# A Macaron layer on one core: the first mixture after two batches' scatters, the late layout between its chunks, the rows written by ScalarE

## The reference

```python
x = x + 0.5 * ffn(layernorm(x))
x = x + attention(layernorm(x))
x = x + 0.5 * ffn(layernorm(x))
# ffn: a mixture of 8 experts, 2 per token
xf = layernorm(x) * ln_g + ln_b
scores, idx = top_k(xf @ router_w, 2); gate = softmax(scores)
# per expert: y = layernorm(xf) * g + b;  x1 = y @ W1 + b1;  x2 = clip(y @ W2 + b2, -20, 20)
# hidden = clip(x1 * x2 * sigmoid(x2), -1e4, 1e4);  out = clip(hidden @ Wo + bo, -1e4, 1e4)
```

## Time and profile before

| | us |
|---|---|
| median of 3 runs | 1285.2 |
| lowest and highest | 1285.19, 1287.82 |
| the profiled execution, whole | 1283.73 |
| its span | 1282.0 |

### The profile page before, as it was taken

One profiled execution on the slowest core, in us unless ns is written; L12 is line 12 of the kernel. 1 busy time (PEld: TensorE's weight loads), 2 busy tenths in 40 slices (PEclk: granted clock), 3 DMA queues, 4 the chain that ended last, 5 costly groups with the idle time before them and its releaser, 6 DMA issues.

```text
span 1282.0 us, 27027 instructions
## 1 busy us (share of the span) xinstructions
PE 1144.8 (89%) x9003; PEld 606.4 (47%) x9003; DVE 1124.8 (88%) x2287; ACT 878.0 (68%) x1849; POOL 518.6 (40%) x672
## 2 busy tenths in 40 slices
PE   3857999888699999999999999999999999999993
PEld 2745888877322222332223223222222367788882
DVE  7877888887799999989999999999999778988885
ACT  1223555555289999898889888898887965455651
POOL 3883556424224001525336333445344128543232
PEclk9999999999689999999999999999999999999997
DMA  8115565563110200012011000010000413555653
GB/s 278 53 63 181 206 204 194 196 238 137 51 51 18 68 18 4 16 31 55 2 31 37 21 18 18 20 42 10 18 9 25 147 72 142 193 206 191 243 200 141
DMA packets 58746, 123.28 MB, mean 96 GB/s; under 512 B 12736, under 2 KB 33954, under 8 KB 58576
## 3 DMA queue, kind: packets, MB, share of 16 engines
q1 hardware_dynamic: 49616, 103.57, 23.6%
q0 software_dynamic: 8704, 16.93, 4.2%
q10 hardware_dynamic: 288, 1.05, 0.2%
HBM read 36.39 MB, written 23.62 MB: 47 GB/s over the span
## 4 chain that ended last, share of the span: by engine, by line
PE 59%; DVE 25%; POOL 6%; issue 5%; DMA 3%; ACT 2%; SPq 1%; DVEq 0%; POOLq 0%; ACTq 0%
PE psum L2329 15%; DVE att_neg_part L1996 13%; PE psum L2301 9%; PE psum L2232 8%; PE psum L2220 7%; PE psum L2222 7%; PE psum L2283 6%; POOL rows_dram L1293 4%; DVE ffn_x2c L1938 2%; DMA ffn_block_rows<-rows_dram 2%; DVE ffn_hidden L1949 2%; DVE stats L1631 1%; PE psum L2307 1%; ACT ffn_silu L1454 1%; PE psum L2172 1%
## 5 line engine op out<-in xcount | busy, mean ns | idle before, releaser
L1996 DVE TENSOR_REDUCE att_neg_part<-psum 128x2 f32<-128x1024 f32 x512 | 594.7, 1215 | 27.0 <-PE psum L2283 24.9
L1486 ACT ACTIVATE att_probs<-psum 128x512 f32<-128x512 f32 x1024 | 556.4, 597 | 59.8 <-PE psum L2301 23.0
L2329 PE MATMUL psum<-att_probs,att_values 128*18 128x256 f32 x4096 | 322.2, 387 | 4.3 <-issue 3.7
L2283 PE MATMUL psum<-att_right,att_left 62*128 62x512 f16 x1024 | 288.1, 391 | 31.0 <-DVE att_neg_part L1996 30.1
L1454 ACT ACTIVATE ffn_silu<-ffn_x2c,ffn_rec 128x256 f32<-128x256 f32 (+1 forms) x320 | 154.7, 487 | 170.4 <-DVE ffn_x2c L1938 169.9
L1309 POOL DMA_INDIRECT y_dram<-ffn_y,ffn_block_rows x144 | 142.6, 990 | 233.9 <-ACT ffn_y L1472 205.5
L2301 PE MATMUL psum<-att_right,att_left 64*128 64x512 f16 x512 | 199.0, 389 | 0.1
L2307 PE MATMUL psum<-att_right,att_left 64*128 64x512 f16 x512 | 194.9, 381 | 0.0
L1938 DVE TENSOR_SCALAR ffn_x2c<-psum,ffn_rec 128x256 f32<-128x256 f32 (+1 forms) x320 | 162.6, 512 | 34.0 <-PE psum L2222 29.7
L2220 PE MATMUL psum<-ffn_block_t,ffn_rec 128*128 128x256 f32 (+1 forms) x640 | 178.7, 361 | 1.8 <-ACT ffn_block_t L1405 1.8
L2222 PE MATMUL psum<-ffn_block_t,ffn_rec 128*128 128x256 f32 (+1 forms) x640 | 178.0, 360 | 0.0
(11 more groups left out here) (236 smaller groups left out, 1040.8 us busy)
## 6 DMA issues: line engine op xcount, KB each, us to landing
ffn_rec<-record SPq DMA_DIRECT2D x80, 776.5 KB, 3.8
ffn_block_rows<-rows_dram SPq DMA_DIRECT2D x64, 130.0 KB, 3.1
record<-in_L_ffn_W SPq DMA_DIRECT2D x16, 256.0 KB, 6.4
att_left<-q_parts_dram SPq DMA_DIRECT2D x64, 64.0 KB, 2.2
att_right<-att_max_parts SPq DMA_DIRECT2D x256, 1.0 KB
y_dram<-ffn_y,ffn_block_rows POOLq DMA_INDIRECT x144, 2.3
x_sb<-in_L_attn_x SPq DMA_DIRECT2D x4, 512.0 KB, 7.1
record<-in_L_ffn_Wo SPq DMA_DIRECT2D x8, 256.0 KB, 7.2
```

The lines of the kernel that those rows point to most:

```text
L1486: S.activation(probs[:, slot % PROBS, :], ring_bank(("score", slot))[:, :], ACT.Exp, scale=unlift).then_inc(att_bank.by_act, 1)
L1996: V.tensor_reduce(out=neg_part[:, h % 2, keys, p::PAIR, t], in_=psum[:, low:high + 1, :], axis=AX.X, op=ALU.max, negate=True).then_inc(red ...
L2283: product = TE.matmul(bank[max_banks(n)[k]], left[s][PRODUCTS[k], p, q], right[s][PRODUCTS[k], p, seen], start=True, stop=True)
L2329: last = TE.matmul(value_bank[g * VS:g * VS + 2 * VW, p * HALF // 2:(p + 1) * HALF // 2], values_flat[:, at:at + 2 * VW], queries, start=( ...
```

## The change

The first mixture starts when the rows of batches 0 and 1 are scattered (`JOBS[0:B - 2]`). The first 9 blocks (`AHEAD`) hold only rows of these two batches: the early layout puts first the whole blocks of `rows_ahead`, and SP waits for batch 2's scatters before it loads block 9. Batch 2's 16 scatters stand at the end of GpSimd's part of the front, and batch 3's remaining ones in slots 0 to 40 of `HEAD`. The late layout moves from the front into `HEAD`, one piece in each of blocks 2 to 10, and the fillers follow it, three a block from block 14 on.

ScalarE writes the rows: `scalar_fill` is 8 activations, one for each tile, Identity with scale rstd and bias -mean * rstd, which VectorE works out as `offset` in one instruction. The semaphore on which the gates wait now counts the fill and the exponent. The pass (x - mean) * ln_g goes from step 0 to step 2, the transposes can start after half of xf, the logits after half of the copies, and the routing uses two PSUM banks per batch in turn. The constants of VectorE stand behind batch 1's statistics. `first_routing` has a new order, written out by batch, folds and scatters included. New buffers and the move of batch 2's and 3's routing buffers behind those of the mixture are left out below, as are unchanged lines.

```diff
@@ -119,6 +119,7 @@
+    AHEAD = -((E * (BLOCK - 1) - TOPK * N * (B - 2)) // BLOCK)
@@ -451,8 +460,9 @@
-        route_bank = [Banks([bank[b]], semaphore(f"route_full{b}"), semaphore(f"route_emptied{b}"))
-                      for b in range(B)]
+        route_banks = [Banks(bank[2 * k:2 * k + 2], semaphore(f"route_full{k}"), semaphore(f"route_emptied{k}"))
+                       for k in range(2)]
+        route_bank = [route_banks[b % 2] for b in range(B)]
@@ -508,7 +518,9 @@
-            return [n for n in range(PLACED + 1) if not (on_pool(job) and n in (XF, FILLED))]
+            if job[0] == 0 and job[1]:
+                return [SHIFTED1, XF_FIRST, XF, SHIFTED2, WON, CHOSEN, LED, FILLED, PLACED]
+            return [n for n in range(PLACED + 1) if not (on_pool(job) and n in (XF, FILLED) or job[0] and n == XF_FIRST)]
@@ -517,8 +529,13 @@
-        def by_act(job, step):
-            return set_of(job).by_act, job[4] * ACT_STEPS + step
+        def rows_by_act(job):
+            return set_of(job).by_act, 1
+        def shared(job):
+            return set_of(job).by_act, 2 + job[4] * ACT_STEPS
@@ -728,10 +745,13 @@
+        OUT_SLOTS = [0, 4, 8, 10, 12, 16, 18, 20, 24, 26, 28, 32, 36, 40]
...
-            HEAD[HC * (n - FIRST_OUT)].append(("route", JOBS[B - 1], ROUTE_STEPS - 1, (n, BT * TOPK)))
+            HEAD[OUT_SLOTS[n - FIRST_OUT]].append(("route", JOBS[B - 1], ROUTE_STEPS - 1, (n, BT * TOPK)))
+        for n in range(9):
+            HEAD[HC * (1 + n) + 2].append(("lay", 1, 0, (n, 9)))
@@ -811,44 +831,60 @@
-            def scatters(b, part):
-                yield "route", JOBS[b], SCATTER, (part, 6)
...
+            def scatter(b, places):
+                for n in places:
+                    yield "route", JOBS[b], SCATTER, (n, BT * TOPK)
...
+            yield "constants", 0, 0, WHOLE
...
+            yield "fill", 0, 0, WHOLE
...
-            yield from folds((0,))
-            for b in range(1, B):
-                yield from steps(b, (2,))
-                yield from folds((3 * b - 2,))
-                yield from scatters(b - 1, 0)
-                yield from steps(b, (3, 4))
-                yield from scatters(b - 1, 1)
-                yield from steps(b, (5,))
-                yield from folds((3 * b - 1, 3 * b))
-                yield from steps(b + 1, (0,))
-                yield from steps(b, (6,))
-                yield from scatters(b - 1, 2)
-                yield from steps(b + 1, (1,))
-                yield from steps(b, (7,))
-                yield from scatters(b - 1, 3)
-                yield from steps(b, (8, 9))
-                if b == B - 1:
-                    yield "folded", 0, 0, WHOLE
-                yield from scatters(b - 1, 4)
-                yield from steps(b, (10, 11))
-                if b == B - 2:
-                    yield "lay", 0, 0, WHOLE
-                yield from scatters(b - 1, 5)
+            yield from folds((0, 1))
+            yield from steps(1, (2, 3, 4))
+            yield from scatter(0, range(0, 5))
+            yield from steps(1, (5,))
+            yield from steps(2, (0,))
+            yield from steps(1, (7, 8, 9, 6))
+            yield from scatter(0, range(5, 7))
+            yield from folds((2, 3))
+            yield from steps(2, (1,))
+            yield from steps(1, (10,))
+            yield "fill", 1, 0, WHOLE
+            yield from steps(1, (11,))
+            yield from scatter(0, range(7, 13))
+            yield from steps(2, (2, 3, 4, 5))
+            yield from steps(3, (0,))
+            yield from steps(2, (7, 8, 9, 6))
+            yield from folds((4, 5, 6, 7))
+            yield from scatter(0, range(13, 15))
+            yield from steps(3, (1,))
+            yield from scatter(0, range(15, 16))
+            yield from steps(2, (10,))
+            yield "fill", 2, 0, WHOLE
+            yield from steps(2, (11,))
+            yield "lay", 0, 0, WHOLE
+            yield "lifts", 0, 0, WHOLE
+            yield from scatter(1, range(0, 14))
+            yield from steps(3, (2, 3, 4, 5))
+            yield from folds((8,))
+            yield "folded", 0, 0, WHOLE
+            yield from steps(3, (7, 8, 9, 6))
+            yield from scatter(1, range(14, 16))
+            yield from steps(3, (10,))
+            yield "fill", 3, 0, WHOLE
+            yield from steps(3, (11,))
+            yield from scatter(2, range(0, 16))
@@ -918,7 +954,7 @@
-                for job in JOBS[0:B - 1]:
+                for job in JOBS[0:B - 2]:
@@ -938,7 +974,7 @@
-            first, some = ((8, 1), (14, 3))[k]
+            first, some = 14, 3
@@ -966,6 +1002,8 @@
+            if k == 0 and i == AHEAD:
+                sync_rows_written(JOBS[B - 2])
@@ -1287,6 +1325,8 @@
+                if k_ffn == 0:
+                    G.wait_ge(*rows_by_act(job))
@@ -1397,6 +1439,14 @@
+        def scalar_fill(b):
+            job, r = JOBS[b], sets[b]
+            S.wait_ge(*by_dve(job, FILLED))
+            for t in range(BT):
+                last = S.activation(r.rows[:, t, :, 0:F], r.xf[:, t, :].unsqueeze(1).to_broadcast([P, TOPK, F]),
+                                    ACT.Identity, bias=r.offset[:, t:t + 1], scale=r.rstd[:, t:t + 1])
+            last.then_inc(r.by_act, 1)
@@ -1413,7 +1463,7 @@
-                for job in JOBS[1:B - 1]:
+                for job in JOBS[1:B - 2]:
@@ -1557,32 +1607,35 @@
+            for what, which, step, part in first_routing():
+                if what == "route":
+                    vector_route(which, step, part)
+                elif what == "constants":
+                    vector_constants()
+                elif what == "lay":
+                    vector_lay_out_early(ahead=rows_ahead)
+                elif what == "lifts":
+                    vector_lifts()
+                elif what == "fold" and which == 0:
+                    vector_square()
+                elif what == "folded":
+                    vector_fold()
+            vector_experts(0)
+            vector_attention()
+            vector_experts(1)
+            vector_last_sums()
+        def vector_constants():
...
-            settle(V.tensor_reduce(out=order[:, :], in_=not_later[:, :, :].rearrange("p i j -> p j i"), axis=AX.X, op=ALU.add))
-            settle(V.memset(running[:, :, :], 1.0))
+            V.memset(running[:, :, 1:BT + 1], 1.0)
...
-            V.memset(ends[:, :, 0:1], 0.0).then_inc(dve_made, 1)
-            V.wait_ge(dve_made, 1)
-            for what, which, step, part in first_routing():
-                if what == "route":
-                    vector_route(which, step, part)
-                elif what == "lay":
-                    vector_lay_out_early()
-                elif what == "fold" and which == 0:
-                    vector_square()
-                elif what == "folded":
-                    vector_fold()
-                    vector_lifts()
-            vector_lay_out_late()
-            vector_experts(0)
-            vector_attention()
-            vector_experts(1)
-            vector_last_sums()
+            V.memset(ends[:, :, 0:1], 0.0)
+            settle(V.tensor_reduce(out=order[:, :], in_=not_later[:, :, :].rearrange("p i j -> p j i"), axis=AX.X, op=ALU.add))
@@ -1634,6 +1687,12 @@
+        def vector_less_mean(r, src, nt):
+            for t in range(nt):
+                last = V.scalar_tensor_tensor(r.xf[:, t, :], src[:, t, :], r.mean_var[:, t, 0:1],
+                                              ln_g_bc[:, :], ALU.subtract, ALU.mult)
+            settle(last)
@@ -1653,20 +1712,20 @@
-                if not on_pool(job):
-                    V.wait_ge(norm_in, 48)
-                    for t in range(nt):
-                        last = V.scalar_tensor_tensor(r.xf[:, t, :], src[:, t, :], r.mean_var[:, t, 0:1],
-                                                      ln_g_bc[:, :], ALU.subtract, ALU.mult)
-                    settle(last)
+                if job == JOBS[-2]:
+                    vector_less_mean(r, src, nt)
...
+                if k_ffn == 0:
+                    V.wait_ge(norm_in, 48)
+                    vector_less_mean(r, src, nt)
...
+                    if t == nt // 2 - 1 and k_ffn == 0:
+                        last.then_inc(r.by_dve, 1)
@@ -1689,6 +1748,10 @@
+                if k_ffn == 0:
+                    V.scalar_tensor_tensor(r.offset[:, :], r.mean_var[:, :, 0], -1.0, r.rstd[:, :],
+                                           ALU.mult, ALU.mult).then_inc(r.by_dve, 1)
+                    return
@@ -1762,7 +1825,7 @@
-                V.wait_ge(*by_act(job, SHARED))
+                V.wait_ge(*shared(job))
@@ -1774,16 +1837,21 @@
-        def vector_lay_out_early(part=WHOLE):
+            if k_ffn == 0 and b == B - 3:
+                V.tensor_tensor(rows_ahead[:, :], carry[0:1, :], region[0:1, :], ALU.subtract)
+        def vector_lay_out_early(part=WHOLE, ahead=None):
...
```

(12 more changed lines are left out.)

20 lines of the change are left out of this document (14 added, 6 removed).

## The result

The changed kernel takes 1297.97 us (median; 1296.75 to 1298.98), beside 1285.78 for the kernel before (1285.19 to 1287.82): a ratio of 1.0089, 95% interval 1.0076 to 1.0101. It is slower by 0.9%. The forecast was 1297.0. The profiled execution of the changed kernel took 1298.54, with a span of 1296.8.

The account below looks back on a forecast made before the run. Bound: the chain of waits to the first mixture matmul, led by GpSimd's row scatters, then TensorE's pace. A first copy 10.6 later plus 1.2 for the late layout, 11.8 on the 1285.2 median, gave 1297.0 us; range 1289 to 1304.

Parts of the forecast that it names:

- The chain: Front, through gates waiting for exponent and fill behind the folds: first copy of block_t at 116.2, 10.6 us later.
- The fill: ScalarE's row writing in the front: 8 activations of 0.50 us each, 4.0 a fill, between 0.45 and 0.58 each.
- Price of a fold: TensorE's folds of expert weights in the front: 3.42 us each, seven of them on the path.
- GpSimd's cover: GpSimd at the mixture's start: row scatters end at 130, first result scatter due near 132, no cost, 2 us to spare.
- The late layout: Nine pieces in blocks 2 to 10: pieces up to about 0.95 us free, larger ones lose their excess; +1.2, between 0 and 3.
- The fillers: Blocks 14 to 16, three at a time on SP's queue: free, since row loads are issued over two blocks ahead.
- Fast folds: Rival, front: four folds in a row bring TensorE to its high level, 1.7 us a fold, time 1285; chance 5%.
- More table loads: Rival, ScalarE's front: a table load of 1.28 us before every fill and exponent from batch 1, 7.7 in all, 1305; chance 5%.
- The plan works: Rival, front: folds are hidden after all, copy starts between 83 and 95, time 1264 to 1277 us; chance 9%.

Follow-up runs that it names:

- Experiment 3: Changed kernel with half of each fold's matmuls left out, waits and order kept: 1287.11 us in a single run.
- Experiment 2: Changed kernel with the late layout back in front of the mixture and the fillers one a block from block 8: 1299.56 us, ratio 1.011.
- experiment 5: Changed kernel with exponent and fill ahead of the folds, fold 8 beside folds 4 to 7, fillers one a block from block 8: 1270.72 us, ratio 0.9895.
- experiment 1: Changed kernel with exponent and fill ahead of folds 2 and 3 in batch 1 and of folds 4 to 7 in batch 2: 1276.02 us, ratio 0.9928.
- fillers alone: Changed kernel with only the fillers set back to one a block from block 8: 1296.44 us, ratio 1.0094.
- experiment 4: Kernel before, with the two folds behind a batch's logits moved behind its tally, ahead of its exponent: 1292.59 us, ratio 1.006.

## Why the prediction was right

The time, the mechanism and the places were right. Three terms of the sum were off by about 1 us each, one of them the other way, so they partly cancel.

- **The chain, step by step.** Chosen of batch 1: 38.6 predicted, its tally follows at 38.53. Folds 2 and 3 to 45.6; the scaling starts at 45.61. Fill at 47.1; it is at 46.76. Batch 2's tally at 64.2; it is at 64.15. Folds to 78.1; the next scaling is at 78.05. Logits of batch 3 done at 102.2; fold 8 begins at 101.18, 1.0 earlier: that is where the 0.9 comes from by which the copy beat its forecast of 116.2 (115.33). I rounded up in batches 2 and 3.
- **The fill** was taken as 0.50 an activation, 4.0, between 0.45 and 0.58. It takes 4.02 to 4.04 for eight. By the Trainium skill, ScalarE: Activation LUTs, section What ACT_TABLE_LOAD costs, the prediction estimated 3.9. That takes the overlap off all eight; eight have seven overlaps, and with these the page's figures give an estimated 4.0, as the rows do.
- **Price of a fold**: 3.42 from the kernel before held through 13.79 us of folds in one run. Experiment 3 shows folds 2 to 8 on the path.
- **GpSimd's cover** of 2: the first result scatter was to be due near 132 with row scatters ending at 130. They end at 129.5, and the scatter of results at 131.39 waited for ScalarE's weighing by 1.86.
- **The late layout**, +1.2, was mis-sized: 2.2. The step that failed is that pieces of up to 0.95 are free, taken from one block of the second mixture with a single piece, which took 5.59. In the changed kernel the first piece takes 0.8 (from 131.15), and the y biases around it stand 6.01 apart instead of 5.62. Experiment 2 shows that without any piece blocks 0 to 11 take 61.8; with them, 64.0.
- **The fillers**, free by the forecast, cost 1.1. The step that failed is that row loads are issued over two blocks ahead; I took that from the order of the program. The trace of the kernel before has them 4.9 us ahead, under one block (experiment 5), and the load that was issued at 202.38 was waited for from 204.4 on.
- **The single-tile blocks** lose another 1.1 between block 22 and the first matmul of the attention, and in its variants on chips of the same kind 0.7 (experiment 1 and the fillers alone) to 2.1 (experiment 3); experiment 4, the kernel before in another order, gains 0.4 there. The transposes' waits for row loads differ by 0.4 in all (6.4 before, 6.8 after). The forecast had nothing there, and no experiment tells the cause.
- **Rivals.** Fast folds: no, a fold stays at 3.42. More table loads: no, the fills of batches 1 and 2 start 0.1 behind the exponent's start and no load stands before them. The plan works: no in this order, but 93.6 and 89.7 in the orders of experiments 1 and 5, inside the 83 to 95 that the rival gave. So the rival's start was there to be had; the order of the lists lost it.

The sum of terms, 9.65 + 2.2 + 1.1 = 13.0, against the forecast's 11.8: the median went up by 12.2. That 1297.0 met 1297.97 within 1.0 owes something to luck, since the misses of -1.0 and +2.1 partly cancel and the 1.7 behind block 17 in the profiled executions does not show in the medians.

## What to carry to other kernels

When a wait is made to include one more instruction of another engine, go up that engine's list and add everything that the instruction stands behind, and whatever that waits for in turn: here a fill of 4.0 came to waits of 9.9 and 16.7. Long work that is only filler belongs behind the short work for which somebody waits, in every engine's list; two moved lines were worth 22 us here. And DMAs without a deadline, issued in bursts on the queue that also issues loads with one, cost as much as they make those loads late.

## What the runs showed of the hardware

The front runs at the lower of TensorE's two levels, though the granted clock is shown as 1.00. A fold's matmul has one column and a fresh weight; 80 in a row take 17.21 us, 0.215 each, 32 in a row 6.96, 0.217 each. The eight transposes right behind the 80 still take 2.18 (row at 74.21 above), as behind 17.9 us of standing still in the changed kernel (95.92). What the higher level gives can be seen in the kernel before, where the same router logits of eight columns take 3.4 for 16 in the front, 0.21 each, and in the second mixture 0.80 for 8, 0.10 each:

```profile
1069.59 0.95 PE L2155 MATMUL psum<-router_sb,xf_t 128*128 128x8 f32 x8
1070.39 0.68 PE L2220 MATMUL psum<-ffn_block_t,ffn_rec 128*128 128x256 f32 x2
```

In experiment 5's kernel TensorE is busy for 17.3 of the 18 us from 56 to 74, nearly all with folds, and the column shows 1.00. The step comes in the mixture's first block, where pairs of wide matmuls start 0.85 apart at first and then 0.43, which is the step from 1.2 to 2.4 GHz, again with 1.00 shown for 91 to 96:

```profile
92.40 1.06 PE L2290 MATMUL psum<-ffn_block_t,ffn_rec 128*128 128x256 f32 x2
93.25 0.97 PE L2292 MATMUL psum<-ffn_block_t,ffn_rec 128*128 128x256 f32 x2
94.06 0.60 PE L2290 MATMUL psum<-ffn_block_t,ffn_rec 128*128 128x256 f32 x2
94.49 0.59 PE L2292 MATMUL psum<-ffn_block_t,ffn_rec 128*128 128x256 f32 x2
```

So the column does not tell at which of the two levels a front like this one runs; the distance of equal matmuls does.

Two of the chips behaved otherwise. On them the kernel before takes 1296 and 1300, and two variants of the changed kernel lose more than that against their own time elsewhere, 29.5 (experiment 5's, 1300.21 and 1270.72) and 32.4 (fillers alone, 1328.8 and 1296.44). Up to 60 us the traces of the same kernel agree within 0.4. Then small instructions, each dependent on the one before, come 0.45 to 0.7 apart on VectorE, where on the other chip it is 0.19. From VectorE's lifts in experiment 5's kernel, first on such a chip, then on another:

```profile
70.41 0.15 DVE L1671 CAST halved<-halved_i 128x1 f32<-128x1 int32 x1 [0.37 <-DVE halved_i L1670]
71.11 0.15 DVE L1672 TENSOR_SCALAR halved<-halved 128x1 f32<-128x1 f32 x1 [0.55 <-DVE halved L1671]
```

```profile
69.58 0.15 DVE L1671 CAST halved<-halved_i 128x1 f32<-128x1 int32 x1
69.77 0.15 DVE L1672 TENSOR_SCALAR halved<-halved 128x1 f32<-128x1 f32 x1
```

At the same time TensorE's folds show gaps of 0.5 to 1.7 and ScalarE one of 12.8, for which the profile names no instruction as releaser, and the first y bias comes at 121.42, 26.5 behind the copy instead of 11.4. From block 10 on the blocks are back at 5.62. What holds the engines back is open. The consequence is not: the order of experiment 5 gains 1% on a chip where the kernel before takes 1285 (ratio 0.9895) and loses 0.5% on one where it takes 1296 (1.0048), so its advantage has to be measured where it is to run.
